# Loading the repeated expert gates pair by pair, ahead of the z stores

## What is computed

```python
x = x + _L0_conv_ref(_ln_c(x), qkv_w, lepe_w, bias_table)       # attention, rolls 0 and 2, summed
t = _to_tokens(x)                                                # (B, H*W, 64)

router_probs = softmax(tn @ router_w + router_b)                 # tn = layer norm of t
top_p, top_i = top_k(router_probs, 2)
top_p = top_p / sum(top_p)
expert_out = einsum("bnd,edc->bnec", tn, expert_w) + expert_b    # 8 experts
t = t + einsum("bnk,bnkc->bnc", top_p, take(expert_out, top_i))
```

## Time and profile before

| | us |
|---|---|
| device time, median of 3 runs | 3749.16 (3746.48 to 3774.52) |
| the profiled execution | 3730.37 |
| its span, first to last instruction | 3728.5 |
| PE busy | 3199.5 (86%) |
| DVE busy | 3190.4 (86%) |
| POOL busy | 2942.7 (79%) |
| ACT busy | 2233.5 (60%) |

### The profile page before, as it was taken

How to read it: one execution, slowest core, us unless ns; L and a number is a source line. 1 busy time by engine, 2 the same in 40 slices (tenths; PEclk the granted TensorE clock), 3 DMA queues, 4 the chain that set the end, 5 groups by cost and what they waited for, 6 DMA issues and landing times.

```text
span 3728.5 us, 203806 instructions
## 1 busy us (share of the span) xinstructions
PE 3199.5 (86%) x82757; PEld 1956.7 (52%) x82757; DVE 3190.4 (86%) x6174; ACT 2233.5 (60%) x4514; POOL 2942.7 (79%) x5385
## 2 busy tenths in 40 slices
PE   3889989988898888898889888888889888989884
PEld 1655555555555555555555555555555555555541
DVE  2789989998999989998889988888889988889983
ACT  2676666666666656665566656665556666666640
POOL 3988878888888878887788878877788878788860
PEclk8999999999999999999899999999899989999996
DMA  1245455555455545555545555545455545455545
GB/s 27 60 97 126 117 123 121 129 120 122 118 127 121 124 109 129 115 127 115 120 110 127 122 117 121 125 111 122 113 120 125 124 115 123 114 116 126 125 104 126
DMA packets 415302, 432.05 MB, mean 116 GB/s; under 512 B 129984, under 2 KB 395888, under 8 KB 414320
## 3 DMA queue, kind: packets, MB, share of 16 engines
q1 hardware_dynamic: 248432, 304.94, 36.0%
q0 software_dynamic: 165888, 113.57, 12.9%
HBM read 245.79 MB, written 58.98 MB: 82 GB/s over the span
## 4 chain that ended last, share of the span: by engine, by line
PE 36%; SPq 23%; issue 15%; DVE 14%; DMA 5%; ACT 3%; POOL 2%; DVEq 0%; ACTq 0%; POOLq 0%
SPq L397 13%; PE bank L628 8%; PE bank L564 7%; DVE lepe L899 4%; SPq L429 4%; PE bank L549 3%; PE bank L641 3%; PE bank L584 2%; SPq L455 2%; DVE gx L887 2%; PE bank L633 2%; DMA gate_rows<-gateT 2%; DVE row_max L907 2%; DMA z<-fin 2%; PE bank L653 2%
## 5 line engine op out<-in xcount | busy, mean ns | idle before, releaser
L504 POOL DMA_DIRECT2D vx<-vt x3072 | 1561.7, 517 | 414.1 <-PE bank L633 403.3
L628 PEld LDWEIGHTS bank<-probT,vx 128*32 128x32 f32 x36864 | 824.6, 189 | 464.5 <-issue 452.8
L628 PE MATMUL bank<-probT,vx 128*32 128x16 f32 x36864 | 886.3, 234 | 159.2 <-issue 144.0
L493 POOL DMA_DIRECT2D kx<-k_sb x1536 | 741.0, 489 | 229.5 <-issue 102.8
L564 PEld LDWEIGHTS bank<-kx,qx 32*32 32x32 f32 x36864 | 584.9, 110 | 443.6 <-issue 441.3
L564 PE MATMUL bank<-kx,qx 32*32 32x64 f32 x36864 | 689.3, 223 | 133.3 <-issue 111.1
L899 DVE SCALAR_TENSOR_TENSOR lepe<-vpad,lepe_sb,lepe 128x384 f32<-128x384 f32 x960 | 673.5, 702 | 0.8 <-issue 0.8
L718 ACT ACTIVATE prob<-prob 128x512 f32<-128x512 f32 x576 | 367.4, 638 | 288.1 <-DVE prob L912 285.0
L887 DVE TENSOR_TENSOR gx<-gate_wide,yn_pair 128x768 f32<-128x768 f32 x384 | 397.4, 1036 | 112.9 <-PE bank L549 62.1
L523 POOL TENSOR_TENSOR lepe_p<-lepe_p,tap_sb 128x384 f32<-128x384 f32 x384 | 434.9, 1133 | 32.7 <-issue 11.3
L912 DVE TENSOR_TENSOR prob<-bank,row_max 128x512 f32<-128x512 f32 x576 | 398.4, 692 | 16.7
(11 more groups left out here) (87 smaller groups left out, 4517.8 us busy)
## 6 DMA issues: line engine op xcount, KB each, us to landing
gate_wide<-gate_rows SPq DMA_DIRECT2D x384, 384.0 KB
vx<-vt POOLq DMA_DIRECT2D x3072, 12.0 KB
kx<-k_sb POOLq DMA_DIRECT2D x1536, 24.0 KB
yn_pair<-yn POOLq DMA_DIRECT2D x384, 96.0 KB
z<-fin SPq DMA_DIRECT2D x1344, 24.0 KB
xs<-in_x SPq DMA_DIRECT2D x96, 192.0 KB
xt<-in_x SPq DMA_DIRECT2D x192, 96.0 KB
z0t<-z SPq DMA_DIRECT2D x192, 96.0 KB
```

The source lines that it names most:

```text
L493: pool.dma_start(kx[to + m:to + C:4, r % 2, m, :], k_sb[at + m:at + C:4, r % 2, :])\
L504: pool.dma_start(vx[to:to + TOK, r % 2, g * 8 + x:g * 8 + 8:2, odd, :], vt[at:at + TOK, r % 2, x::2, :, :].rearrange("p h n k -> p h (n k)"))\
L628: last = MM(bank_o[32 * c:32 * c + 32, at * TOK:(at + 1) * TOK], vx[:, kr % 2, :, at % 2, at // 2 * 4 + c], probT[:, kr % 2, at, c * TOK:( ...
```

## The change

The gate loads are cut the other way and moved. Where four DMAs at slot 41+6k each brought all four expert pairs of one quarter of the tile, now eight DMAs bring one pair each to one half of the partitions: two for pair 0 in slot 40+6k, two for pair 1 in slot 41+6k, two for pair 2 in slot 42+6k, two for pair 3 in slot 43+6k. Each is 64 partitions x 2 x 384 numbers (192 KB); the bytes in all are the same. The blocks `store_gates` and `spread_gates` now stand behind `load_pair` and ahead of `store_z` inside a slot. The wait for all products of the tile before is now one wait per pair: pair p waits only for the product p of tile k-1. `GATE_DMAS` goes from 4 to 8, so that product 0 on DVE waits for all eight. Nothing changes on DVE, PE, ACT and POOL but that count.

```diff
-    take_logits=34, gates=36, gap_exp=37, turn_gates=38, pair_yn=38, store_gates=39, spread_gates=41,
+    take_logits=34, gates=36, gap_exp=37, turn_gates=38, pair_yn=38, store_gates=39, spread_gates=40,
-        X_DMAS, Z_DMAS, TILE_DMAS, K_DMAS, V_DMAS, GATE_DMAS = 5, 11, 7, 8, 16, 4
+        X_DMAS, Z_DMAS, TILE_DMAS, K_DMAS, V_DMAS, GATE_DMAS = 5, 11, 7, 8, 16, 8
                     load_pair(r, s.image(r, IMT))
+                if ti := s.tile("store_gates"):
+                    k, r = ti
+                    wait_alone(sp, gateT_saved, k + 1)
+                    if s.later(r, 2):
+                        wait_alone(sp, gate_spread[r % 2], k // 2 * (GATE_DMAS * 16))
+                    sp.dma_start(gate_rows[r % 2], gateT[:, r % 2, :]).then_inc(gate_stored[r % 2], 16)
+                if (ti := s.in_tile("spread_gates")) and ti[2] < PAIRS:
+                    k, r, p = ti
+                    if p == 0:
+                        wait_alone(sp, gate_stored[r % 2], (k // 2 + 1) * 16)
+                    if s.later(r, 1):
+                        wait_alone(sp, gx_made, (k - 1) * PAIRS + p + 1)
+                    by_expert = gate_rows[r % 2].rearrange("(f p e) n -> e p f n", f=2, e=2)
+                    for odd in range(2):
+                        sp.dma_start(gate_wide[odd * C:(odd + 1) * C, p, :, :],
+                                     by_expert[odd, p].unsqueeze(0).broadcast_to([C, 2, SPX]))\
+                            .then_inc(gate_spread[r % 2], 16)
                 if st := s.strip("store_z"):
...
-                if ti := s.tile("spread_gates"):
-                    k, r = ti
-                    wait_alone(sp, gate_stored[r % 2], (k // 2 + 1) * 16)
-                    if s.later(r, 1):
-                        wait_alone(sp, gx_made, k * PAIRS)
-                    by_expert = gate_rows[r % 2].rearrange("(f p e) n -> e f p n", f=2, e=2)
-                    for odd in range(2):
-                        for half in range(2):
-                            sp.dma_start(gate_wide[odd * C:(odd + 1) * C, :, half, :],
```

More of the change, by code:

```diff
@@ L439, in slot @@
                     put(z2t, slice(C, 2 * C), 0, z_flat[1], t * (2 * SP) + SP - ROLL, SP)
-                if ti := s.tile("store_gates"):
-                    k, r = ti
[L442 to L446, removed]
-                if ti := s.tile("spread_gates"):
-                    k, r = ti
-                    wait_alone(sp, gate_stored[r % 2], (k // 2 + 1) * 16)
-                    if s.later(r, 1):
-                        wait_alone(sp, gx_made, k * PAIRS)
-                    by_expert = gate_rows[r % 2].rearrange("(f p e) n -> e f p n", f=2, e=2)
-                    for odd in range(2):
-                        for half in range(2):
-                            sp.dma_start(gate_wide[odd * C:(odd + 1) * C, :, half, :],
-                                         by_expert[odd, half].unsqueeze(0).broadcast_to([C, PAIRS, SPX]))\
-                                .then_inc(gate_spread[r % 2], 16)
                 if ti := s.tile("tile_out"):
```

## The result

The changed kernel takes 4830.26 us (median of 4 runs, 4796.13 to 4836.82) beside 3747.82 for the kernel before: a ratio of 1.285, interval 1.277 to 1.294. The forecast was 4420 with a range to 4720. The direction and the chain of waits came out as forecast; one term of the sum, the landing of pair 3, did not.

What follows compares the result with a forecast made beforehand. No engine owned the chain of waits (PE 36%, SP's issuing 23%). 72 tiles x 45.4 + 17 x 44.2 = 4020 us against 3325, less 25, gave +670 on 3730.4, 4400; with 18.8 for the median 4420, range 4200 to 4720.

Steps and rivals of the forecast that it cites:

- What bounds the kernel, and that pair 3 decides: No engine owns the waits before; after, product 0 waits for pair 3's loads behind z stores and xs: 23.2 us against 14.2.
- Fin end to end of xs: On SP, from the end of slot 42's fin through z stores, their landing and load_tile to xs issued: 18.5 us.
- the wait before pair 3: SP's wait instruction between the issue of xs and pair 3's loads: 0.2 us.
- Landing of the pair: From the first issue of pair 3's loads until they have landed for product 0: 4.5 us, bounds 2.5 and 7.0.
- Product 0 to the next fin: DVE's second stretch of a tile, priced at its mean busy time, 22.2 us; bounds 21.3 and 25.3.
- Rival B: PE idles in the stall, its clock drops, product 0 to fin takes 25.3 us: 4695 us; chance 0.17 for 4560 to 4800.
- Eight loads for four: SP issues eight gate loads at 0.62 us each, 5.0 us a tile for 2.7: +2.3 us.
- SP's own work: SP's work for a tile changes by +0.3 us: more load issues, less the 2.0 us wait for the gate store's landing.
- waits per pair: SP's waits for each product of the tile before, ahead of that pair's loads: cost nothing, as DVE is already past them.
- The sum: Over 89 tiles +695 us, last four tiles -25: 4400 for the profiled execution; 18.8 more for the median, forecast 4420.
- The chances: Probabilities given to the outcomes: slower by more than about one per cent 0.95, faster 0.03, within one per cent 0.02.
- where queue and clock go wrong together: The outcome above 4800 us, with both the DMA queue and PE's clock worse than forecast: chance 0.04.

## Why the prediction was wrong

- *What bounds the kernel, and that pair 3 decides*: right. The chain fin, z stores, landing, load_tile, xs, pair 3, product 0 is in the chain of waits; moving pair 3 out of it alone turned 4830 us into 3662, and moving the wait to product 3 gave 3959, within 30 us of what the same chain gives.
- *Fin end to end of xs, 18.5 us, and the wait before pair 3, 0.2*: right, 19.2 together in the tile shown and 18.4 in the mean of tiles 2 to 89.
- *Landing of the pair, 4.5 us, bounds 2.5 and 7.0*: this step failed. It measured 9.24 us in the tile shown and 9.1 in the mean, above the high bound. I took its price from gate loads near the pipeline's end. Those have no xs load ahead of them, since xs has by then been loaded to the last strip. I did write that xs is still on its way in the same queue, but I allowed for its bytes and not for how few DMA engines carry its 62 rows. With the same rows cut into 48 and 14 the landing is 4.6 us, the term as forecast. So the whole of the excess, 4.6 us a tile, is the wait behind the 62 rows.
- *Product 0 to the next fin, 22.2 us*: right, 22.6 in the eight tiles and 22.0 in the mean of tiles 2 to 89, but partly by luck, as the reason given was another. DVE was busy for 20.1 of the 22.6 and not 22.2, and idle for 2.5. Two of the eight windows (the third column from the right is the clock):

```profile
758.40:779.00 20.60, 19.07 (x515) 11.33 (x515) 19.87 (x38) 11.22 (x23) 11.16 (x23) 0.90 0.31 76
...
3267.60:3290.30 22.70, 19.78 (x441) 10.96 (x441) 20.03 (x38) 11.25 (x22) 11.02 (x23) 0.77 0.33 86
```

  Rival B's cause did occur: the clock was 0.75 to 0.90 in these eight, and the stretch is 2.1 us longer at 0.77 than at 0.90. Its price was met by a gain I had not seen: POOL does much of its work inside the stall now (19.1 us of it in the first stretch, 11.5 in the second, where the earlier trace rows have 20.9), and DVE meets POOL's additions less often. DVE's busy time fell from 3190.4 to 3070.3 us, and the largest part of that is its tap products, as the page of before and then of after has them:

```profile
L899 DVE SCALAR_TENSOR_TENSOR lepe<-vpad,lepe_sb,lepe 128x384 f32<-128x384 f32 x960 | 673.5, 702 | 0.8 <-issue 0.8
```

```profile
L900 DVE SCALAR_TENSOR_TENSOR lepe<-vpad,lepe_sb,lepe 128x384 f32<-128x384 f32 x960 | 595.0, 620 | 0.0
```

- *Eight loads for four, SP's own work, waits per pair*: no part of the result of the change, as foretold, since SP stands idle for fin 1271 us in all (who, for whom, us, times, longest):

```profile
SPq L289 <- DVE fin L959: 1271.2, 169, 13.8
```

  In versions without the chain SP's work does count: the one with pair 3 in slot 42 has 61% of its chain on SP. With four loads in two slots it is 2% and the time 68 us less, though those two kernels differ in the place of the loads too.
- *The sum*: for the profiled execution it gave 4400, and 4828.8 was measured. Of the 429 us between them 398 are the 89 cycles, nearly all of it the landing. The rest is the two ends: behind the fin of tile 89 I put 25 us less, but that stretch grew from 155.1 to 165.4 us, because product 0 of tiles 90 and 91 waits 6.7 and 17.8 us where it waited 0 and 9.3; up to the fin of tile 0 it is 5 us shorter. The 18.8 us that I added for the median came to 1.5, so in the median the two misses nearly cancel.
- *The chances*: slower by over 1% had 0.95. The part above 4800, "where queue and clock go wrong together", had 0.04. It took the queue alone, and 0.04 was too little for a term whose nearest rows came from a place without the neighbour that mattered.

## What to carry to other kernels

When a load moves behind other work in a queue, follow the chain from the event that releases the first thing ahead of it to its first user, and compare that length with the time the user has; here 27.5 us stood against 14.2. Price its landing by a row with the same DMAs in flight ahead of it, and look at how many rows those have, as well as how many bytes. When loads are moved, keep them ahead of any long wait of the engine that issues them, and leave room between a store and the load that reads it back; here that room was worth 5 us a tile.

## What the runs showed of the hardware

How many rows a load has decides how long the loads behind it in SP's queue wait. The same 186 KB of xs (62 rows of 3072 bytes), in the mean of tiles 2 to 89:

| rows of each load | SP issues xs | the packets of 2304 bytes | pair 3 lands after |
|---|---|---|---|
| 48 and 14 | 3.7 us | 2.5 us | 4.6 us |
| 62 | 2.3 us | 7.1 us | 9.1 us |
| 31 and 31 | 5.3 us | 10.4 us | 9.2 us |

gate_rows, issued right behind, lands after a median of 2.9, 7.4 and 7.5 us. It is easily missed, because in the changed kernel xs itself is waited for only once, for 1.6 us; its slowness shows in what is issued behind it.

DVE's tap products of 128x384 numbers slow down where they meet an addition of POOL, and not where POOL issues DMAs. Both cases stand close together in the kernel before, on DVE and on POOL (L504 is POOL's issuing of DMAs, L523 its additions):

```profile
2845.63 0.57 DVE L899 SCALAR_TENSOR_TENSOR lepe<-vpad,lepe_sb,lepe 128x384 f32<-128x384 f32 x1
2849.65 1.90 DVE L899 SCALAR_TENSOR_TENSOR lepe<-vpad,lepe_sb,lepe 128x384 f32<-128x384 f32 x1
```

```profile
2842.96 5.06 POOL L504 DMA_DIRECT2D vx<-vt  x10
...
2850.12 2.29 POOL L523 TENSOR_TENSOR lepe_p<-lepe_p,tap_sb 128x384 f32<-128x384 f32 x2
```

Over that whole trace the 194 of them that overlap such an addition take 1141 ns in the mean, the other 766 take 590. In the changed kernel it is 88 at 899 ns and 872 at 592: the mean falls from 702 to 620 because fewer meet, and those that meet take less long. DVE's transposes of the scores (L972) show no such loss: 704 ns without an overlap and 699 with one, in 88 cases. What the two engines share is not shown by these traces.
